# Group-means product moved from behind the tenth to behind the twelfth pair of the second convolution

## The reference, cut to what matters

```python
x = _conv2d(x, conv1_w, conv1_b)          # 3 -> 64 channels, 3x3
residual = x
x = _group_norm(x, gn1_g, gn1_b)          # 32 groups of 2 channels, over the patch
x = jax.nn.gelu(x, approximate=False)
x = _conv2d(x, rconv1_w, rconv1_b)        # 64 -> 64, 3x3
x = _group_norm(x, gn2_g, gn2_b)
x = jax.nn.gelu(x, approximate=False)
x = _conv2d(x, rconv2_w, rconv2_b)
x = residual + x
x = _conv2d(x, proj_w, proj_b, stride=P, pad=0)   # 16x16 patch -> 192 numbers
```

## Time and profile before

| | |
|---|---|
| median of 3 runs | 1460.72 us |
| the profiled execution's own time | 1465.48 us |
| its span | 1463.7 us |
| TensorE matmul busy | 1365.6 us, 93% of the span |
| VectorE busy | 1081.5 us, 74% |
| ScalarE busy | 864.3 us, 59% |
| GpSimd busy | 576.4 us, 39% |

### The profile page before, as it was taken

One profiled execution on the slowest core, in us unless ns is written; L12 is line 12 of the kernel. 1 busy time (PEld: TensorE's weight loads), 2 busy tenths in 40 slices (PEclk: granted clock), 3 DMA queues, 4 the chain that ended last, 5 costly groups with the idle time before them and its releaser, 6 DMA issues.

```text
span 1463.7 us, 38493 instructions
## 1 busy us (share of the span) xinstructions
PE 1365.6 (93%) x14042; PEld 1022.2 (70%) x14042; DVE 1081.5 (74%) x4148; ACT 864.3 (59%) x2127; POOL 576.4 (39%) x1116
## 2 busy tenths in 40 slices
PE   4999988888999999999999999999999978998889
PEld 2865653344888688858976897788688867754647
DVE  3864358898888988888888889888988854544520
ACT  1434446777667777777767767767777630344451
POOL 1100035555544544544554554544545521162600
PEclk9999999999999999999999999999999988998999
DMA  7799945545554455455545554555455589300000
GB/s 218 208 268 275 266 118 162 183 127 132 139 151 134 128 150 143 131 140 143 147 125 142 150 149 119 147 152 138 128 154 136 149 226 255 79 1 1 1 1 17
DMA packets 125178, 206.17 MB, mean 141 GB/s; under 512 B 20028, under 2 KB 88188, under 8 KB 124478
## 3 DMA queue, kind: packets, MB, share of 16 engines
q1 hardware_dynamic: 124990, 203.71, 51.0%
HBM read 103.11 MB, written 20.70 MB: 85 GB/s over the span
## 4 chain that ended last, share of the span: by engine, by line
PE 63%; DMA 9%; issue 7%; DVE 7%; POOL 6%; SPq 6%; ACT 2%; POOLq 0%; ACTq 0%; DVEq 0%
PE rc L637 26%; PE pj_st L728 8%; DMA sb_acts<-sb_hst 7%; PE rc L638 6%; PE pj_st L732 4%; POOL sb_tmp L487 4%; PE rc L658 3%; PE rc L657 3%; DMA sb_wall_arena<-scratch_fold 2%; SPq L372 2%; SPq L311 2%; PE c L693 2%; DVE sb_bn L952 1%; PE rc L1440 1%; PE rc L1528 1%
## 5 line engine op out<-in xcount | busy, mean ns | idle before, releaser
L637 PE MATMUL rc<-sb_acts,sb_rwd 128*64 128x512 f16 x1764 | 559.3, 390 | 17.4 <-DMA sb_acts<-sb_hst 17.4
L638 PE MATMUL rc<-sb_acts,sb_rwd 128*64 128x512 f16 x1764 | 560.3, 390 | 0.0
L487 POOL TENSOR_TENSOR sb_tmp<-sb_mst,sb_half_neg 128x8 f32<-128x8 f32 x200 | 350.7, 1754 | 456.3 <-DVE sb_mst L973 453.4
L554 ACT ACTIVATE sb_f32q<-c,sb_gsh,sb_gsc 128x128 f32<-128x128 f32 x792 | 298.7, 458 | 273.7 <-POOL sb_gsh L497 273.7
L637 PE MATMUL rc<-sb_acts,sb_rwl 128*64 128x512 f16 x1176 | 361.8, 389 | 0.0
L638 PE MATMUL rc<-sb_acts,sb_rwl 128*64 128x512 f16 x1176 | 361.1, 389 | 0.0
L728 PE MATMUL pj_st<-sb_wall_arena 128*64 128x384 f16 x1792 | 308.6, 334 | 6.9 <-DVE sb_wall_arena L992 6.6
L576 ACT ACTIVATE sb_g2f<-rc,sb_gsh,sb_gsc 128x128 f32<-128x128 f32 x784 | 298.1, 481 | 4.5 <-POOL sb_gsh L497 4.5
L732 PEld LDWEIGHTS pj_st<-sb_wall_arena 128*64 128x64 f16 x1792 | 221.6, 221 | 62.3
L732 PE MATMUL pj_st<-sb_wall_arena 128*64 128x192 f16 x1792 | 242.8, 245 | 0.0
L728 PEld LDWEIGHTS pj_st<-sb_wall_arena 128*64 128x64 f16 x1792 | 218.8, 218 | 22.7 <-DVE sb_wall_arena L992 6.7
(11 more groups left out here) (191 smaller groups left out, 1856.3 us busy)
## 6 DMA issues: line engine op xcount, KB each, us to landing
sb_acts<-sb_hst SPq DMA_DIRECT2D x792, 78.8 KB, 2.6
sb_im<-x_planes SPq DMA_DIRECT2D x202, 136.5 KB
sb_wall_arena<-w_lo SPq DMA_DIRECT2D x48, 528.0 KB, 3.9
sb_acts<-sb_hst SPq DMA_DIRECT2D x96, 162.0 KB, 3.2
sb_wall_arena<-w_lo SPq DMA_DIRECT2D x24, 480.0 KB, 3.7
sb_f32q<-in_proj SPq DMA_DIRECT2D x12, 576.0 KB, 4.8
sb_wall_arena<-in_proj SPq DMA_DIRECT2D x12, 576.0 KB, 5.2
w_lo<-sb_wall_arena SPq DMA_DIRECT2D x8, 768.0 KB, 3.7
```

The costliest lines, as they stand in the source:

```text
L487: ch.did(gp.tensor_tensor(t1, var, half_neg[:, :], ALU.pow))
L554: ins = nc.scalar.activation(g1f[:, q * Q + m, :], c1[q][:, m * HALF:(m + 1) * HALF], ACT.Gelu, bias=gsh[q][:, m:m + 1], scale=gsc[q][:, m ...
L637: nc.tensor.matmul(out[0:CH, :], w_odd, x_odd, start=(n == 0), stop=(n == 14))
L638: yield nc.tensor.matmul(out[CH:128, :], w_even, x_even, start=(n == 0), stop=(n == 14))
```

## The change

In each slot the means product (with its wait for the moments) is put behind pair 12 of the convolution instead of behind pair 10. `MEANS_AT` is used in `emit` alone. The order of the woven projection steps, the place of `conv1` behind pair 13 and all other engines' programs stay as they are.

```diff
-MEANS_AT, CONV1_AT = 10, 13
+MEANS_AT, CONV1_AT = 12, 13
```

## The result

The changed kernel takes 1477.03 us (median of 4 runs, 1476.75 to 1478.68) where the kernel before took 1461.78 beside it. The ratio is 1.0091, with a 95% interval from 1.0051 to 1.0131: slower by 0.9%. The profiled execution took 1476.85 us with a span of 1474.7; that of before 1465.48 with 1463.7. So the two traces are 11.0 us apart, the medians 15.2.

What follows compares the result with a forecast made beforehand. TensorE was taken to bound the 144 projecting slots, VectorE the other 52. Costs of 6.1 + 3.8 + 4.7 + 0.6 = 15.2 us on the 1460.7 us median gave 1475.9, forecast as 1475.8 us; 8-in-10 range 1462 to 1488 us.

Steps and rivals of the forecast that it cites:

- The shift: How much later TensorE reaches the means product: 0.56 us with ten projection steps, 0.66 with twelve, 0.47 without projection.
- VectorE in the projecting slots: In the 144 slots where TensorE sets the time, VectorE's whole round moves later with the product, at no cost.
- `conv1` and the gelu: In projecting slots the gelu moves 0.56 us against a margin of 0.61 before `conv1`'s weight load; 0.05 left, cost nothing.
- The copies in the projecting slots: Copies issued later reach pair 7 late in 19 tight even slots, each costing the shift less its margin: 6.1 us.
- Group 0: First group, without projection: VectorE resumes 0.47 us later in each of eight slots where it waits for the product: 3.8 us.
- The heads: First slots of groups 2 to 6, without projection: two parts, 2.8 and 1.9 us, together 4.7 us, between 0 and 8.0.
- The first part: VectorE leaves the projecting slots 0.56 us later, coming out at pair 7 of the head's fourth slot: 5 x 0.56 = 2.8 us.
- The second part: In four of five heads the first slot also waits at pair 7 for copies: 4 x 0.47 = 1.9 us.
- The loop's end: From the last read of the means through the last copies to the next stage's loads: 0.56 later, 0.6 us.
- The landing: When copies arrive after issue: 4.9 us by the profile row, which was followed; 2.2 us by the Trainium skill's page.
- The landing rival: Other packets, not the issue, set when copies land: 3 us or less added, 1461 to 1464 us; chance 0.13.
- Faster: Rival: pairs done inside TensorE's wait for the moments end it 0.47 us earlier; at most 9 us gained, 1452 us; chance 0.07.

## Why the prediction was right, and where its terms were off

The forecast of 1475.8 us, 1.0% slower, met a measured 0.91% and 0.84%. What hangs on the product, and that the copies and the heads would pay while VectorE's delay would not, was right; the path in the heads and the make-up of the copies' term were not. By its own steps:

- **The shift.** Right. In the stalled slot of group 0 that answers to the earlier trace rows, pair 7 starts at 260.95 and VectorE goes on at 262.64, 1.69 us later, where it was 262.11 - 260.89 = 1.22: 0.47 more, as worked out. The first of the two in the timeline of the changed kernel:

```profile
260.95 0.41 PE L637 MATMUL rc<-sb_acts,sb_rwd 128*64 128x512 f16 x1 [1.44 <-DMA sb_acts<-sb_hst]
```

and VectorE's:

```profile
262.64 0.19 DVE L968 TENSOR_REDUCE sb_mst<-pj_st 128x16 f32<-128x32 f32 x1 [1.38 <-PE pj_st L702]
```

- **VectorE in the projecting slots.** Right: idle 0.45 us, at no cost, shown by the pair with light patch loads.
- **`conv1` and the gelu.** Right, and by as little as stated: 0.05 to 0.12 us of the margin are left and no projecting slot is longer for it; one pair more and it binds. In the first slot of a head it did bind (below).
- **The copies in the projecting slots.** The size was right (6.1 forecast; 5.3, 5.3 and 4.9 measured), its make-up was not, so part of that agreement is luck. I took 19 short margins that each give a little (counted again from the landings of the trace they are 17, slots 50 to 188, and give 5.4 us). The time from the copies' issue to pair 7 did shrink by a median of 0.54 us, the shift. But nine slots gave 0.11 to 1.44 us each, and three of them (68, 186, 190) had margins of 0.9 to 1.2 us. The landing of the last copy varies in one and the same slot: in slot 190 it took 5.5 us from its issue in the first trace of the changed kernel and 3.5 in the second. So a margin under some 1 us is a chance of a wait and no cover; which slots pay changes from execution to execution, and only their sum stays near 5 us. Likewise I said that waits of pair 7 would be many more and longer by 9 us in all; they became 34, then 39 in the second trace, for 29, and 4.2 and 7.1 us longer. In the second trace's list:

```profile
PEld rc L637 <- DMA sb_acts<-sb_hst: 35.6, 39, 2.8
```

- **Group 0.** Eight times 0.47 gave 3.8 us. The odd slots, whose copies are in time, show the cost: where VectorE goes on late behind a late copy, the `conv1` of the next slot is late. Slots 3, 7, 11, 15, 19 and 25 are longer by 0.45, 0.49, 0.45, 0.45, 0.29 and 0.51 us, and by the same within 0.04 in the second trace. With slots 1, 13 and 17 the odd slots make 3.4 and 3.9 us, and 3.1 in the kernel that is late only without projection; with the program unchanged they make 0.6, two slots of it behind a halved clock. So the size was right. The count was right by luck: three of the eight waits lie in the first two slots and only five stand behind a late copy, but nine odd slots pay, most 0.3 to 0.5 us. Whether the even slots give any of it back, by a shorter wait for the copies, isn't settled. They move by more than the term: with one and the same program slot 10 took 1.7 us more and slot 14 0.9 us less in one trace than in the other. Of the 1.7, 1.1 come ahead of pair 7, through the landing, and 0.6 behind it, where the clock was halved. The whole group, against its unchanged program, grew by 1.5 and 0.9 us only. So "nothing absorbs that 0.47" stays in doubt.
- **The heads.** 4.7 forecast for groups 2 to 6; 2.9 and 4.2 in two traces, and 2.6 with the copies in time. The first part, 5 x 0.56, has the right size (0.51 to 0.54 a head with the copies in time), but the step to it failed: VectorE's delay was to come out "at pair 7 of that slot", the fourth, "through the copies". It comes out in the first slot, at `conv1`, which waits for the gelu, also where no copy is late, so it is the gelu's path and not the copies'. In the changed kernel's two traces slot 56 is 0.54 and 0.52 us longer and slot 168 0.53 both times; in the other three the first slot moves with its landing. The second part is shown by the kernel with the product late only outside the projecting slots: 0.35, 0.35, 0.35 and 0.23 in the second slots, 1.3 us for the 1.9 forecast.
- **The loop's end.** From the last `conv1` of the loop to the first matmul of the next stage it is 0.4 and 0.5 us more in the two traces, for 0.6.
- **The landing.** The kernel with light patch loads settles it: what a late copy waits for are the patch loads ahead of it, by their bytes, as the number of packets is the same. Between 600 and 620 us the longest landing is 3.2 us with light loads and 5.6 with full ones. The landing rival was right that other transfers make the copies late, and falls by its cost: with the copies tight, the projecting slots lost 5 us, not next to nothing, since those transfers are issued later too. The Trainium skill's rule ("DMA: Bandwidth & Descriptors", section "Anatomy of one DMA — SWDGE (gpsimd) path"), an estimate of 2.2 us, agrees with the median of 2.1 with light loads, and not with the 5.6 behind full ones; the projecting slots' 5.3 us that it would have left out are there.
- **Faster.** TensorE's wait for the moments shrank from 40.5 to 28.0 us, and the kernel was slower. With the light loads it shrank too, from 49.4 to 29.3 us, and the heads were still 0.53 longer (line numbers are one higher there). With pair 10:

```profile
PEld pj_st L703 <- DVE sb_ms L965: 49.4, 54, 3.3
```

With pair 12:

```profile
PEld pj_st L703 <- DVE sb_ms L965: 29.3, 53, 3.7
```

The measured sizes (means of the two traces, group 0 by its odd slots, the loop's end at its lower value) make 3.7 + 3.6 + 5.3 + 0.4 = 13.0 us, 0.89%, between the two measured ratios. The forecast's 15.2 equals the difference of the first medians, and that is luck in part: each of its terms is somewhat large, and the second pair of medians is 11.4 us apart. "About 1466 to 1484", called the range from the bounds of the terms, doesn't follow from them: the bounds stated add up to about 1461 and 1527 us.

## What to carry to other kernels

Move an instruction in steps to both sides and measure each place: the time falls to a floor between two walls (here the moments at pair 8, the gelu and the copies above 10), and the margins of single slots tell beforehand where the walls are. A hidden delay is free only on the paths whose margin covers it; look for the path with the most variable end, here a transfer queued behind larger loads (136.5 KB each, two ahead of copies of 78.8 KB), because it pays first, and count a margin smaller than that variation as a chance and not as cover. Compare slots by the start of the same instruction in both traces; a stretch of fixed times holds other work once anything ahead of it has moved. Before an experiment reorders a queue, work out the deadline of the transfer that is moved back, and what the instruction it now stands behind waits for.

## What the runs showed of the hardware that was not expected

- With the same program in it, the stage ahead of the loop took from 192.6 to 202.7 us to the first `conv1` among the traces (before 197.6, after 195.8). Up to 200 us TensorE's weight loads waited 18.9 us for copies, eight times, in the slowest of them, and 10.8 us, three times, in the fastest; from 180 to 200 us its granted clock was 0.91 and 1.00 (mean shares of 2.4 GHz). So single traces of this kernel can be compared by stages only.
- Group 0 varied by 3.5 us between two traces in which its program is the same, through the landing of the copies and through stretches of 3.4 us at half the full clock (granted 0.50), of which the one trace has two there and the other none.
- A patch load of 16 of its 1294 numbers per row instead of all of them took 1.3% off the whole kernel, the largest gain seen here (some 1.0% in the loop, by the traces). Packets stayed at 125178 and bytes fell from 206.17 to 178.84 MB: the bytes of the loads ahead, and not the copies' own or the number of packets, made the landing late.
